# Routed weights of two experts read in 32x32 blocks and turned on VectorE, with low parts and one-hot products at other places

## What is computed

```
x = x + tanh(g_xattn) * attention(layernorm(x), ctx, ctx)        # 16 heads of 16
h = layernorm(x)                                                  # 4096 rows of 256
p = softmax(h @ gate_w.T)                                         # 4 experts
w = the two largest of p, divided by their sum; comb = w at the places of these two, else 0
y = sum over e of comb[:, e] * (silu(h @ eg[e].T) * (h @ eu[e].T)) @ ed[e].T      # 688 wide
y = y + silu(h @ sg.T) * (h @ su.T) @ sd.T                        # shared expert, 688 wide
x = x + tanh(g_ffn) * y
```

## Time and profile before

| | |
|---|---|
| median of 3 runs | 883.38 us (883.05 to 883.73) |
| the profiled execution | 881.68 us, its span 879.9 us |
| mean granted TensorE clock | 0.992 of full |
| TensorE busy (matmul) | 846.5 us, 96% |
| VectorE busy | 581.9 us, 66% |
| ScalarE busy | 520.8 us, 59% |
| GpSimd busy | 461.2 us, 52% |
| DMA | 62.05 MB in 56887 packets |

### The profile page before, as it was taken

The page is one execution under the profiler, slowest core; times in us unless marked ns, Lnnn a source line. Parts: engine busy times, 40 slices in busy tenths (PEclk is TensorE's granted clock), DMA queues, the critical chain, the costliest instruction groups (busy, mean ns, idle before and its releaser), DMA issues.

```text
span 879.9 us, 19161 instructions
## 1 busy us (share of the span) xinstructions
PE 846.5 (96%) x6271; PEld 742.7 (84%) x6272; DVE 581.9 (66%) x1203; ACT 520.8 (59%) x1846; POOL 461.2 (52%) x551
## 2 busy tenths in 40 slices
PE   8788999999999999999999999999999999999995
PEld 7566788888888799999988888888888888889994
DVE  6899899999998577876564555555555545444442
ACT  4999999999999444656464444444445444322221
POOL 6686767667565353676531454444443444364442
PEclk9899999999999999999999999999999999999998
DMA  7125233322313222333240333222222232232221
GB/s 219 42 77 180 68 90 94 90 66 90 90 66 96 73 74 85 120 103 103 86 141 25 49 49 49 43 41 38 41 41 42 47 48 37 31 49 42 36 40 20
DMA packets 56887, 62.05 MB, mean 71 GB/s; under 512 B 15642, under 2 KB 45183, under 8 KB 56799
## 3 DMA queue, kind: packets, MB, share of 16 engines
q1 hardware_dynamic: 42871, 43.15, 15.8%
q0 software_dynamic: 12864, 17.57, 12.7%
q10 hardware_dynamic: 1064, 0.21, 0.1%
HBM read 34.78 MB, written 25.82 MB: 69 GB/s over the span
## 4 chain that ended last, share of the span: by engine, by line
PE 85%; ACT 5%; DVE 5%; issue 2%; DMA 1%; POOL 1%; DVEq 0%; SPq 0%; ACTq 0%; POOLq 0%
PE p_s L623 23%; PE p_f L640 12%; PE p_f L2767 9%; PE p_s L341 6%; PE p_f L2812 5%; PE p_s L2767 4%; ACT prob L1484 4%; PE p_t L2698 3%; PE p_t L352 3%; PE p_s L2684 3%; PE p_m L2725 3%; PE p_m L2665 2%; PE p_m L2713 2%; PE p_s L2812 2%; PE p_s L2870 1%
## 5 line engine op out<-in xcount | busy, mean ns | idle before, releaser
L509 POOL DMA_INDIRECT out_rows<-big_yout,slot_id x52 | 86.6, 1666 | 158.2 <-DVE big_yout L586 146.3
L1484 ACT ACTIVATE prob<-p_s,negmax 128x77 f32<-128x77 f32 x512 | 161.1, 372 | 7.2 <-DVE negmax L2032 7.0
L537 ACT ACTIVATE big_sil<-p_s 128x512 f32<-128x512 f32 (+1 forms) x78 | 46.6, 597 | 144.7 <-PE p_s L623 126.1
L1484 ACT ACTIVATION_READ_ACCUMULATOR prob<-p_s,negmax 128x1 f32 x512 | 128.9, 255 | 0.0
L569 DVE TENSOR_TENSOR big_hid<-p_s,big_sil 128x512 f32<-128x512 f32 (+1 forms) x78 | 54.0, 692 | 99.5 <-ACT big_sil L537 88.5
L623 PE MATMUL p_s<-big_fxT_hi,big_w_hi 128*128 128x512 f32 (+1 forms) x286 | 113.8, 398 | 0.3 <-ACT big_w_hi L529 0.3
L623 PE MATMUL p_s<-big_fxT_lo,big_w_hi 128*128 128x512 f32 (+1 forms) x286 | 112.7, 394 | 0.0
L623 PE MATMUL p_s<-big_fxT_hi,big_w_lo 128*128 128x512 f32 (+1 forms) x286 | 112.2, 392 | 0.0
L1108 POOL TENSOR_TENSOR prob<-prob,rinv 128x616 f32<-128x616 f32 x64 | 78.5, 1236 | 62.1 <-DVE rinv L2039 62.1
L1127 POOL TENSOR_TENSOR shT_lo<-shid,shT_hi 128x256 fp32r<-128x256 f32 x80 | 63.0, 800 | 44.4 <-ACT shT_hi L1526 44.3
L640 PE MATMUL p_f<-wd_hi,big_hT_hi 128*128 (+1 forms) x312 | 85.5, 280 | 0.0
(11 more groups left out here) (341 smaller groups left out, 2537.7 us busy)
## 6 DMA issues: line engine op xcount, KB each, us to landing
xr<-in_x SPq DMA_DIRECT2D x16, 256.0 KB, 2.9
x_scratch<-xr SPq DMA_DIRECT2D x16, 256.0 KB, 2.8
xn_scratch<-xn SPq DMA_DIRECT2D x16, 256.0 KB, 2.1
xt_scratch<-xnT SPq DMA_DIRECT2D x16, 256.0 KB, 3.2
xin<-xt_scratch SPq DMA_DIRECT2D x16, 256.0 KB, 3.6
x1in<-x_scratch SPq DMA_DIRECT2D x16, 256.0 KB, 3.3
out_rows<-syout SPq DMA_DIRECT2D x16, 256.0 KB, 2.2
raw<-in_L_ffn_ed SPq DMA_DIRECT2D x4, 688.0 KB, 4.3
```

The costliest lines, as they stand in the source:

```text
L509: pool.indirect_dma_start(out, bass.IndirectOffsetOnAxis(slot_id[:, column(j, t)], 0), yout[:, t, :], None, compute_op=ALU.add).then_inc(s ...
L1484: last = act.activation(prob[n % 2][t][:, m * PW + h * SK:m * PW + (h + 1) * SK], p_s[:, 2 * t + h // 4, col:col + SK], ACT.Exp, bias=negm ...
```

## The change

For experts 0 and 1 (FLIPS = 2, matrices 0 to 5) TensorE no longer turns anything. `load_turned` loads the matrix so that whole 32x32 blocks lie where the turned matrix has them: for each quarter a of the partitions (32 rows) and each block of 128 columns one DMA whose elements are 32 floats (128 bytes). A gate or up matrix takes 4 x (2 + 1) = 12 DMAs with 5632 such pieces, a down matrix 4 x 6 = 24 with 6144. VectorE's transpose, which turns each 32x32 block by itself, then gives the turned matrix: `flip(q, part)`, two parts per matrix, writes it in float32 into the place of the low part; for gate and up the last 32 columns (which overlap the 16 before the end) are a second, chained transpose. ScalarE copies it to the high part (`flip_hi`), and the low part is that in place less the high part (`flip_lo`): on GpSimd for matrices 0, 1 and 5, on VectorE for 2, 3 and 4.

So per engine, in the late units:

- TensorE: e_T(0) to e_T(21) are gone. spread(0) to (7) move: before they stood at the ends of units 10, 11 and 12, in 12, 13, 14 and 14; now in 10; 11 (two); 12 (two); 13 (two); 14, the last ahead of down(13).
- ScalarE: e_hi(0) to (21) are replaced by twelve flip_hi.
- VectorE: e_lo(0) to (21) are replaced by twelve flips (units 8, 8, 8, 8, 10, 10, 11, 11, 12, 12, 13, 13) and six flip_lo (units 10, 11, 12). places, rows_at and experts_of_tiles move.
- GpSimd: tails(0) and (1) are gone, six flip_lo come (0 and 1 in units 8 and 9, 5 in unit 14); row_ids and low_shares move.
- SP: matrix 2 is issued after unit 8's load of rows, as before, and now waits for flip(0, 1); matrices 3 to 7 after units 9, 11, 12, 13, 14 (before 10, 10, 11, 12, 13).
- In the first small tile, two of the last block's results come before x_lo(1) and two after.

```diff
+TURN = 32
+FLIPS = 2
+TURNED = 2 * 3 * FLIPS
+WHOLE = FF // TURN * TURN
+SIDE = WHOLE + TURN
+def load_turned(eng, v, raw, s_raw, q):
+    n, kind = q // 3, "gud"[q % 3]
+    src = v["e" + kind][n]
+    for a in range(P // TURN):
+        rows = raw[a * TURN:(a + 1) * TURN, :]
+        if kind == "d":
+            for c in range(FC):
+                at = c * P + a * TURN if c < FC - 1 else CUT + a % 2 * TURN
+                eng.dma_start(rows[:, c * H:(c + 1) * H].rearrange("p (b x) -> p b x", x=TURN),
+                              src[:, at:at + TURN].rearrange("(b r) x -> r b x", r=TURN)).then_inc(s_raw, 16)
+        else:
+            blocks = rows[:, 0:KC * SIDE].rearrange("p (k b x) -> p k b x", k=KC, x=TURN)
+            for k in range(KC):
+                at = k * P + a * TURN
+                eng.dma_start(blocks[:, k, 0:WHOLE // TURN, :],
+                              src[0:WHOLE, at:at + TURN].rearrange("(b r) x -> r b x", r=TURN)).then_inc(s_raw, 16)
+            eng.dma_start(blocks[:, :, WHOLE // TURN, :],
+                          src[FF - TURN:FF, :].rearrange("r (k a x) -> a r k x", a=P // TURN, x=TURN)[a]
+                          ).then_inc(s_raw, 16)
...
-            if isinstance(j, int) and j == 0:
-                last_results()
+            first = isinstance(j, int) and j == 0
+            if first:
+                last_results(0)
             if not last:
                 x_lo(j + 1)
+            if first:
+                last_results(1)
...
+        def turned_part(q, part, s):
+            e, kind = q // 3, "gud"[q % 3]
+            if kind == "d":
+                n = FC // 2
+                return ewd[s][:, e * FC + part * n:e * FC + (part + 1) * n, :].rearrange("p c h -> p (c h)")
+            o = 0 if kind == "g" else FF
+            return ewgu[s][:, e * KC + part, o:o + FF]
...
-        AFTER_UNIT = {2: 8, 3: 10, 4: 10, 5: 11, 6: 12, 7: 13, 8: 15, 9: 15, 10: 15, 11: 16}
+        FIRST_G = PER * FLIPS
+        AFTER_UNIT = {2: 8, 3: 9, 4: 11, 5: 12, 6: 13, 7: 14, 8: 15, 9: 15, 10: 15, 11: 16}
...
                 if q < 2:
                     sp.wait_ge(s_wtr, PER)
+                elif q < 2 + 3 * FLIPS:
+                    sp.wait_ge(s_flip, 2 * (q - 1))
                 else:
-                    sp.wait_ge(s_etr, groups_before(q - 1))
-                load_matrix(sp, v, raw[q % 2], s_raw[q % 2], q)
+                    sp.wait_ge(s_etr, groups_before(q - 1) - FIRST_G)
+                (load_turned if q < 3 * FLIPS else load_matrix)(sp, v, raw[q % 2], s_raw[q % 2], q)
...
+            def flip_lo(q, part):
+                pool.wait_ge(s_ehi, 2 * q + part + 1)
+                low = turned_part(q, part, 1)
+                pool.tensor_tensor(low, low.bitcast(fp32), turned_part(q, part, 0), ALU.subtract).then_inc(s_fliplo, 1)
...
+            def flip_hi(q, part):
+                act.wait_ge(s_flip, 2 * q + part + 1)
+                if q == 0 and part == 0:
+                    act.wait_ge(s_Wo, NU)
+                    act.wait_ge(s_xb, NU)
+                act.activation(turned_part(q, part, 0), turned_part(q, part, 1).bitcast(fp32),
+                               ACT.Copy).then_inc(s_ehi, 1)
...
+            def flip(q, part):
+                dve.wait_ge(s_raw[q % 2], raw_count(q))
+                dst = turned_part(q, part, 1).bitcast(fp32)
+                if q % 3 == 2:
+                    n = FC // 2 * H
+                    last = nc.vector.transpose(dst, raw[q % 2][:, part * n:(part + 1) * n])
+                else:
+                    at = part * SIDE
+                    nc.vector.transpose(dst[:, 0:WHOLE], raw[q % 2][:, at:at + WHOLE]).then_inc(s_flipped, 1)
+                    dve.wait_ge(s_flipped, 4 * (q // 3) + 2 * (q % 3) + part + 1)
+                    last = nc.vector.transpose(dst[:, FF - TURN:FF], raw[q % 2][:, at + WHOLE:at + SIDE])
+                last.then_inc(s_flip, 1)
```

The order of ScalarE and VectorE in units 8 and 9 (VectorE to last_lo(9)); the first is ScalarE:

```diff
                 gate(8, 0)
-                e_hi(0)
+                flip_hi(0, 0)
                 xn_hi(9)
                 gate(8, 1)
-                e_hi(1)
+                flip_hi(0, 1)
                 h_hi(8, 0)
                 h_hi(8, 1)
-                e_hi(2)
                 gate(8, 2)
                 gate(8, 3)
                 h_hi(8, 2)
+                flip_hi(1, 0)
                 gate(8, 4)
-                e_hi(3)
                 h_hi(8, 3)
                 gate(8, 5)
-                e_hi(4)
+                flip_hi(1, 1)
                 h_hi(8, 4)
                 h_hi(8, 5)
...
                 inner(8, 0)
+                flip(0, 0)
                 inner(8, 1)
-                e_lo(0)
-                e_lo(1)
+                flip(0, 1)
                 chosen()
                 result(7)
                 ranks()
                 shares()
                 inner(8, 2)
-                e_lo(2)
+                flip(1, 0)
                 inner(8, 3)
                 weights()
                 inner(8, 4)
-                e_lo(3)
                 counts()
+                flip(1, 1)
                 inner(8, 5)
-                e_lo(4)
 
                 last_lo(8)
                 starts()
...
                 position(1)
-                e_lo(5)
                 inner(9, 4)
                 tiles_and_rows()
                 inner(9, 5)
-                e_lo(6)
+                places(0)
 
                 last_lo(9)
```

More of the change, by code:

```diff
@@ L1354, in late_units @@
                 h_lo(8, 0)
+                flip_lo(0, 0)
                 h_lo(8, 1)
+                flip_lo(0, 1)
                 h_lo(8, 2)
                 h_lo(8, 3)
+                flip_lo(1, 0)
                 h_lo(8, 4)
@@ L1361, in late_units @@
                 h_lo(9, 0)
+                flip_lo(1, 1)
                 h_lo(9, 1)
@@ L1791, in late_units @@
                 h_hi(9, 4)
-                e_hi(7)
                 h_hi(9, 5)
@@ L2497, in late_units @@
                 inner(9, 5)
-                e_lo(6)
+                places(0)
                 last_lo(9)
-                e_lo(7)
+                rows_at(0)
                 inner(10, 0)
+                flip(2, 0)
                 inner(10, 1)
-                places(0)
-                rows_at(0)
                 places(1)
+                flip(2, 1)
                 result(9)
-                e_lo(8)
                 inner(10, 2)
-                e_lo(9)
                 rows_at(1)
                 inner(10, 3)
-                e_lo(10)
+                flip_lo(2, 0)
@@ L2514, in late_units @@
                 inner(10, 4)
+                flip_lo(2, 1)
                 inner(10, 5)
+                last_lo(10)
                 places(2)
-                last_lo(10)
-                e_lo(11)
+                inner(11, 0)
                 rows_at(2)
-                experts_of_tiles()
-                inner(11, 0)
-                e_lo(12)
-                inner(11, 1)
-                result(10)
-                inner(11, 2)
-                e_lo(13)
-                inner(11, 3)
-                inner(11, 4)
@@ L2530, in late_units @@
-                inner(11, 5)
-                places(3)
-                last_lo(11)
-                e_lo(14)
-                rows_at(3)
-                inner(12, 0)
-                inner(12, 1)
-                places(4)
-                rows_at(4)
-                result(11)
-                inner(12, 2)
-                e_lo(15)
-                inner(12, 3)
-                e_lo(16)
-                e_lo(17)
-                inner(12, 4)
-                inner(12, 5)
-                last_lo(12)
@@ L2550, in late_units @@
-                e_lo(18)
-                places(5)
-                inner(13, 0)
-                e_lo(19)
-                inner(13, 1)
-                result(12)
-                rows_at(5)
-                places(6)
-                inner(13, 2)
-                rows_at(6)
+                inner(11, 1)
+                flip(3, 0)
+                result(10)
+                flip(3, 1)
+                inner(11, 2)
+                places(3)
+                inner(11, 3)
+                rows_at(3)
@@ new lines, in late_units @@
+                inner(11, 4)
+                flip_lo(3, 0)
+                inner(11, 5)
+                flip_lo(3, 1)
+                last_lo(11)
+                places(4)
+                inner(12, 0)
+                rows_at(4)
+                inner(12, 1)
+                flip(4, 0)
+                result(11)
+                flip(4, 1)
+                inner(12, 2)
+                flip_lo(4, 0)
+                inner(12, 3)
+                places(5)
+                inner(12, 4)
+                rows_at(5)
@@ L2560, in late_units @@
+                inner(12, 5)
+                flip_lo(4, 1)
+                last_lo(12)
+                places(6)
+                inner(13, 0)
+                rows_at(6)
+                inner(13, 1)
+                flip(5, 0)
+                result(12)
+                flip(5, 1)
```

(23 more changed lines are left out.)

149 lines of the change are left out of this document (63 added, 86 removed).

## The result

The changed kernel takes 891.9 us (median; 889.6 to 893.2) against 883.4 (882.2 to 884.0) beside it: ratio 1.0094, 95% interval 1.0075 to 1.0113, 8.6 us slower. The forecast was 882.1, with 875.5 to 888.5 as its range. The profiled execution took 892.5 us, its span is 890.8.

What follows compares the result with a forecast made beforehand. TensorE, busy 96% of the span, was taken to bound the kernel. Terms 3.9 - 5.9 + 1.5 - 0.8 gave -1.3 us, so the median of 883.38 becomes 882.1; range 875.5 to 888.5, the forecast's own 879 to 885.

Steps and rivals of the forecast that it cites:

- Units 10 to 14. TensorE bounds again: After down(9) TensorE bounds again: 5.9 us of transposes gone against 3.9 late, -2.0, plus 1.5 for the second down matrix.
- down(9): Unit 9: down(9) starts 3.9 us late, at 361.1, with unit 10's rows loaded behind 24 DMAs.
- late second matrix: Units 10 to 14: second down matrix lands near 407.5, flip(5,0) waits some 6 us; priced 1.5, between 0 and 5.
- Rival E: Units 10 to 13: GpSimd with its one-hot products keeps their old length, all given back, 883.4 us; chance 0.02.
- TensorE, -10.0 - 1.1: Late units: removed transposes of both experts save 10.0 us, and a 1.1 us wait of e_T(8) for VectorE goes.
- rival C: VectorE transpose slower than a compare: a flip 1.1 us more, four in units 8 and 9, 886.6 us; chance 0.08.
- down(8): Unit 8: down(8) starts at 344.4 instead of 342.23, +2.2, behind VectorE's chain with the new flips.
- GpSimd's low parts: Units 8 and 9: 2.1 us each on GpSimd, costing nothing, or 2 if down(8) has to wait for one.
- SP: SP's queue: DMAs 0.46 us apart, 11.0 for a down matrix, 5.5 for gate or up; xn_hi(10) near 349.8.
- Packets: Block loads on SP: 128-byte packets, 6144 per down matrix, were left behind the DMA issues, at no added cost.
- Rival B: Block loads dear on SP or in the engines: slower from 0.54 us each, 887.5 at 0.60, 897 at 0.74; chance 0.19.
- Transition: Change from blocks to small tiles: TensorE's 0.78 us wait for x_lo(1) goes, -0.8 (0 to -0.8).

Runs made afterwards that it cites:

- c2: Changed kernel with low parts moved to units 14 and 15, one-hot products at their old places and SP's order mended: 880.7 us, ratio 0.9972.
- L: Edit to the changed kernel: low parts of experts 0 and 1 moved out of units 8 to 12; alone 894.5 us, ratio 1.0131.
- S: Edit to the changed kernel: SP's order mended, urgent loads and stores ahead of a matrix's blocks, second expert's up and down matrices earlier; alone 890.3 us.
- e10_hotnew: Changed kernel with low parts moved to units 14 and 15 and SP's order mended, one-hot products at their new places: 887.6 us, ratio 1.0050.
- H: Edit to the changed kernel: one-hot products back at the places of the kernel before; alone 890.4 us, ratio 1.0091.
- e12_hot_sp: Changed kernel with one-hot products at their old places and SP's order mended, low parts left where the change put them: 886.3 us, ratio 1.0046.
- e6_lows_hot: Changed kernel with all ten low parts moved to units 14 and 15 and one-hot products at their old places: 891.5 us, ratio 1.0090.
- e1_lows_late: Changed kernel with GpSimd's four low parts of units 8 and 9 moved to unit 15: 894.0 us, ratio 1.0122.
- e3_plain: Changed kernel with block-wise loads of the first six matrices replaced by two plain loads each (weights arrive unsorted): 889.9 us, ratio 1.0081.
- e11_sp_only: Changed kernel with only SP's order mended: 890.3 us, ratio 1.0088.
- e4_split: Kernel before with only the last block's last results split in two halves around x_lo of the next small tile: 883.6 us, ratio 1.0008.
- e2_hot_old: Changed kernel with all one-hot products back at the places they had before: 890.4 us, ratio 1.0091.
- e5_lows_all: Changed kernel with all ten low parts of units 8 to 12 moved to units 14 and 15: 894.5 us, ratio 1.0131.
- e7_lows_hot_plain: Changed kernel with low parts in units 14 and 15, one-hot products at old places, two plain loads per matrix (weights unsorted): 881.7 us, ratio 0.9990.
- e9_plain24: Changed kernel with low parts late, one-hot products at old places, block loads replaced by as many plain DMAs (weights unsorted): 889.7 us, ratio 1.0068.
- c1: Changed kernel with low parts late, one-hot products at old places, and unit 10's rows loaded ahead of the first down matrix: 890.3 us, ratio 1.0080.

## Why the prediction was wrong

**The step that failed** is "Units 10 to 14. TensorE bounds again". Down(9) was 4.2 us late where 3.9 was forecast; from there to down(14) the forecast was -5.9 + 1.5 = -4.4, and it came out at +4.8: 9.2 of the 10.0 us between the forecast and the result. The waits of TensorE between them sum to 8.2 us (0.35, 0.62, 2.20, 0.64, 0.99, 1.29, 2.12) against 0.7 before, the second fall of the clock costs 1.7, and the thirteen groups gave 5.1: 8.2 - 0.7 + 1.7 - 5.1 = 4.1; the other 0.7 I can't place. Of the 8.2, 3.5 are for GpSimd's shT_lo (0.35, 2.20, 0.99) and 4.7 stand ahead of one-hot products, 2.12 of them behind the late second matrix. Rival E had the mechanism, GpSimd with its one-hot products, but stopped at "given back" and had a chance of 0.02. The timeline of GpSimd in unit 11 of the changed kernel shows its part, and the same place in the kernel before stands behind it:

```profile
383.33 1.10 POOL L1372 TENSOR_TENSOR at_val<-at_til,ids 128x544 fp32r<-128x544 f32 x1
384.39 1.23 POOL L1172 TENSOR_TENSOR shT_lo<-shid,shT_hi 128x256 fp32r<-128x256 f32 x1
385.58 1.09 POOL L1377 TENSOR_TENSOR at_val<-at_til,w_lo 128x544 fp32r<-128x544 f32 x1
386.63 1.71 POOL L1172 TENSOR_TENSOR shT_lo<-shid,shT_hi 128x256 fp32r<-128x256 f32 x1
388.31 1.73 POOL L1372 TENSOR_TENSOR at_val<-at_til,ids 128x544 fp32r<-128x544 f32 x1
390.00 1.37 POOL L1172 TENSOR_TENSOR shT_lo<-shid,shT_hi 128x256 fp32r<-128x256 f32 x1
391.34 1.27 POOL L1377 TENSOR_TENSOR at_val<-at_til,w_lo 128x544 fp32r<-128x544 f32 x1
392.57 1.20 POOL L1172 TENSOR_TENSOR shT_lo<-shid,shT_hi 128x256 fp32r<-128x256 f32 x1
```

```profile
384.62 1.31 POOL L1127 TENSOR_TENSOR shT_lo<-shid,shT_hi 128x256 fp32r<-128x256 f32 x1 [0.92 <-ACT shT_hi L1526]
385.89 1.28 POOL L1327 TENSOR_TENSOR at_val<-at_til,ids 128x544 fp32r<-128x544 f32 x1
387.13 2.08 POOL L1332 TENSOR_TENSOR at_val<-at_til,w_lo 128x544 fp32r<-128x544 f32 x1
```

In the changed kernel there is no gap, four products of 128x544 stand between the h_lo, and the last h_lo ends as down(11) starts (393.83). I had counted the one-hot products, eight before and eight after, and not where on GpSimd they stand: before, two of four came behind the unit's last h_lo. A shorter unit on TensorE leaves the other engines less time, so a count that stays equal is not neutral: even in c2, with the products where they were, TensorE waits 1.17 us for shT_lo at down(12), where it waited for nothing before.

The placing is one of three parts. From down(9) to down(14) it is 75.6 us before and 80.4 in the changed kernel (71.2 forecast), 79.5 with L and S mended (e10_hotnew), 75.1 with H and S (e12_hot_sp), 78.4 with L and H (e6_lows_hot), and 73.4 with all three (c2). With the two others gone, the new places cost 6.1 us of it and SP's order 5.0 (1.7 of each is clock), and VectorE's low parts 1.7.

Step by step:
- **TensorE, -10.0 - 1.1.** From down(10) to down(11), with two spreads and no wait in either, it was 386.68 - 371.74 = 14.94 before and 387.02 - 373.19 = 13.83 in c2, for three groups less: 0.37 each, not 0.44. 22 groups are 8.2 to 8.6 (0.39 in the next unit, c2's wait of 1.17 taken out), so this term was some 1.6 too large. The two starts that I read right behind a group gave more than a whole unit does; why is not shown.
- **Flips** 0.87 + 0.21 (672 and 32 columns) and 0.97 (768): right; rival C is out. The estimate of 1.6 us for 672 columns that I worked out from the Trainium skill ("VectorE: DVE Perf Modes", The three transpose paths) doesn't hold for these 32-bit blocks.
- **bases** +0.4: it was 0.0. **down(8)** +2.2: it was 4.4. The missing 2.2 is "GpSimd's low parts ... nothing, or 2 if down(8) has to wait for one": the second value had the size, not the way. They did not hold down(8) by their length, 1.7 us each, but by what they do to VectorE, 2.8 us (e1_lows_late). The Trainium skill says so ("SBUF — State Buffer", Who interferes with whom): a VectorE instruction with two SBUF inputs and a GpSimd one that reads SBUF exclude each other. The trace agrees for the 128x32 products, 0.92 against 0.27 us; a cast with one input was stretched too (0.66 against 0.20). I had not weighed that page.
- **SP.** 24 DMAs in 11.0 us: 11.7 measured. Gate or up 5.5: 8.4, 0.70 each. The rows of unit 10, xn_hi(10) 4.9 late: 5.1. down(9) +3.9: 4.2. The queue was read rightly, but that down(9) met its number is in part luck: with the rows in time it comes no earlier, 34.5 us after down(7) in e3_plain and 33.7 in e11_sp_only against 33.3 in the changed kernel, since down(8), 2.2 us later than forecast, and the clock loss behind it hold it as well. With down(8) mended it is still 32.5 (e1_lows_late), against 28.7 before: there the rows decide. The late second matrix was right: flip(5,0) waited 2.3 us (6 forecast), spread(7) 2.12 (below); priced 1.5, worth 1.7 in the changed kernel (18.9 us from down(12) to down(13) against 17.2 in e11_sp_only; 0.5 of it is clock) and 5.1 with L and H mended (e6_lows_hot against c2).
- **Packets** of 128 bytes: left behind the issues, right. By the Trainium skill a transfer needs 512 bytes or more to run at full rate ("DMA: Bandwidth & Descriptors", Specifications); here a DMA takes 0.49 us with 128 bytes and 0.46 with 1 KB. Rival B had a threshold of 0.54 us each. The first down matrix stays below it (0.49), the second is at it (0.55) and gate and up above (0.70), so B's prices were partly there. By themselves they did not make the kernel slower: with two plain loads a matrix it still takes 889.9 us (e3_plain), and with SP's order mended the blocks cost nothing that shows (c2).
- **Transition** -0.8: 0.0, given back (e4_split).
- **Not in the sum:** the clock, 3.4 us: half of it in unit 9, half in the step that failed. I had forecast some 9 us of waits in units 8 and 9 (5.13 and 1.14 at the two downs, 0.74 at bases came) and treated a wait as costing its length.

```profile
414.96 0.98 DVE L2145 STREAM_TRANSPOSE wd_lo<-raw 128x768 f32<-128x768 f32 x1 [2.34 <-DMA raw<-in_L_ffn_ed]
...
420.33 0.72 DVE L2502 TENSOR_TENSOR at_til<-iota_til,til_f 128x544 f32<-128x544 f32 x1
```

## What to carry to other kernels

Where an engine at 96% is relieved, the others get less time for the same work: lay out for each of them what the next stage waits for, in order, not only the sum. Bounds that stand side by side hide one another: here three repairs gave under 2 us each and 11 together, so a repair that shows nothing is no proof that its cause is absent. A wait of TensorE can cost more than its length: look at the granted clock behind it before pricing it. Many DMAs on one queue cost what stands behind them; issue the urgent loads first, and the bulk as early as its buffer is free.

## What was not expected of the hardware

- GpSimd's low parts (128x688, SBUF to SBUF, 1.7 us) stretch VectorE's small instructions by 0.46 to 0.65 us each, five of them by 2.8 us. A transpose of 128x672 beside one (338.90) takes 0.87 us as elsewhere.
- It goes the other way as well. GpSimd's instructions from 320 to 440 us took, over the shortest of the same line and shape in the execution, 9.6 us more before and 15.2 in the changed kernel. A least-squares fit of that excess to what VectorE ran at the same time gives, for each us in the changed kernel, 0.57 us beside the comparisons that make at_til and at_row, 0.62 beside VectorE's flip_lo and 0.11 beside the transposes, and in the kernel before none beside the e_lo that read PSUM. A fit, not a test.
- The granted clock: in or right behind waits of 5.1 us at down(8) it fell to half each time (changed, e2_hot_old, e3_plain, e11_sp_only, e12_hot_sp). After one of 2.3 us at the same place it fell in e1_lows_late and e5_lows_all, and not in e6_lows_hot, e7_lows_hot_plain, e9_plain24, c1, c2 and e10_hotnew, with the same waits before it. Each fall took 1.5 to 3.1 us. What decides at such a wait these runs don't show.
